# Down weights with four neighbouring rows per partition, gate and up columns taken in the matching order

## The reference

```python
def _swiglu_ffn(x, wg, wu, wd):
    return jax.nn.silu(x @ wg) * (x @ wu) @ wd
...
top_w, top_i = jax.lax.top_k(probs, K)            # K = 6 of E = 64
gate = jnp.zeros((N, E), dtype=x.dtype).at[jnp.arange(N)[:, None], top_i].set(top_w)
for e in range(NS):                               # NS = 2 shared experts
    shared = shared + _swiglu_ffn(x, sWg[e], sWu[e], sWd[e])
for e in range(E):
    routed = routed + _swiglu_ffn(x, Wg[e], Wu[e], Wd[e]) * gate[:, e:e + 1]
out = (shared + routed + x)
```

## Time and profile before

| | us |
|---|---|
| median of 3 runs | 1272.34 (1271.11 to 1272.39) |
| profiled execution | 1267.19 |
| its span | 1265.8 |
| TensorE busy in the span | 980.7 (77%) |
| VectorE busy | 568.4 (45%) |
| DMA queue q1 (SyncE): share of the 16 DMA engines | 55.0% |
| mean rate of all DMAs | 255 GB/s |

### The profile page before, as it was taken

How to read it: one execution, slowest core, us unless ns; L and a number is a source line. 1 busy time by engine, 2 the same in 40 slices (tenths; PEclk the granted TensorE clock), 3 DMA queues, 4 the chain that set the end, 5 groups by cost and what they waited for, 6 DMA issues and landing times.

```text
span 1265.8 us, 20487 instructions
## 1 busy us (share of the span) xinstructions
PE 980.7 (77%) x7256; PEld 520.0 (41%) x7257; DVE 568.4 (45%) x1367; ACT 228.8 (18%) x582; POOL 372.2 (29%) x421
## 2 busy tenths in 40 slices
PE   0166757667676666776889999999899996999986
PEld 0023423333243332433654545455354543545463
DVE  5266859577595866996441111111111121111116
ACT  1021202122120321212311211112111120212100
POOL 1724041340414315000167322333223232232110
PEclk9997878887786978898577999999999997999998
DMA  7926061551605426056367999999999999999937
GB/s 245 326 73 253 15 266 62 205 202 66 266 34 232 155 113 261 6 200 226 130 196 245 318 391 381 387 393 384 392 384 389 390 379 399 384 382 388 371 106 205
DMA packets 92476, 322.76 MB, mean 255 GB/s; under 512 B 18395, under 2 KB 18548, under 8 KB 70322
## 3 DMA queue, kind: packets, MB, share of 16 engines
q1 hardware_dynamic: 68080, 259.90, 55.0%
q0 software_dynamic: 22432, 57.44, 12.9%
q10 hardware_dynamic: 1826, 3.54, 0.9%
HBM read 310.15 MB, written 13.63 MB: 256 GB/s over the span
## 4 chain that ended last, share of the span: by engine, by line
PE 67%; issue 11%; DVE 8%; DMA 3%; DVEq 3%; ACT 3%; another core or an unknown queue 2%; POOL 1%; SPq 1%; ACTq 0%; POOLq 0%
PE ps L1081 19%; PE ps L575 13%; PE ps L1125 10%; DVE big L558 5%; PE ps L1151 4%; PE ps L609 3%; PE ps L1031 3%; PE ps L625 3%; PE ps L1100 2%; PE ps L593 2%; DMA big<-y_d 2%; PE ps L1169 2%; DVEq L556 2%; PE ps L1075 1%
## 5 line engine op out<-in xcount | busy, mean ns | idle before, releaser
L558 DVE TENSOR_TENSOR big<-big 128x512 f32 x640 | 392.0, 694 | 156.7 <-remote 110.5
L575 PE MATMUL ps<-big,mixed 128*32 128x256 f32 x2560 | 219.5, 436 | 144.0 <-issue 97.0
L1081 PE MATMUL ps<-big 128*64 128x512 f32 x1024 | 248.2, 629 | 28.3 <-issue 27.2
L317 POOL DMA_INDIRECT big<-xn_d,idx x160 | 154.7, 967 | 342.8 <-DVE big L558 271.5
L575 PEld LDWEIGHTS ps<-big,mixed 128*32 128x32 f32 x2560 | 90.0, 121 | 266.0 <-issue 173.9
L1091 DVE TENSOR_TENSOR mixed<-big,ps 128x256 f32<-128x256 f32 x64 | 27.0, 421 | 295.3 <-ACT big L1088 291.3
L1081 PEld LDWEIGHTS ps<-big 128*64 128x64 f32 x1024 | 71.3, 144 | 163.5 <-issue 163.5
L1125 PE MATMUL ps<-big,mixed 128*64 128x256 f32 x1024 | 128.0, 393 | 1.6 <-issue 1.6
L981 POOL DMA_INDIRECT big<-h_d,Lg x52 | 50.9, 979 | 260.4 <-issue 258.9
L1048 POOL DMA_INDIRECT y_d<-big,sia x74 | 75.5, 1020 | 107.7 <-DVE big L1138 62.9
L584 ACT ACTIVATE mixed<-ps 128x512 f32<-128x512 f32 x40 | 23.9, 598 | 385.4 <-PE ps L575 359.9
(11 more groups left out here) (191 smaller groups left out, 728.7 us busy)
## 6 DMA issues: line engine op xcount, KB each, us to landing
big<-in_L_ffn_Wg SPq DMA_DIRECT2D x64, 1024.0 KB
big<-in_L_ffn_Wu SPq DMA_DIRECT2D x64, 1024.0 KB
big<-in_L_ffn_Wd SPq DMA_DIRECT2D x64, 1024.0 KB
big<-in_edge_attr SPq DMA_DIRECT2D x10, 4096.0 KB
big<-y_d SPq DMA_DIRECT2D x10, 672.0 KB
big<-xn_d,idx POOLq DMA_INDIRECT x160
big<-in_L_ffn_sWg SPq DMA_DIRECT2D x2, 1024.0 KB, 5.0
big<-in_L_ffn_sWu SPq DMA_DIRECT2D x2, 1024.0 KB, 7.1
```

Of the source, the lines that this page charges most:

```text
L317: pool.indirect_dma_start(xs[s][:, c, :], None, xn_d[:, :], bass.IndirectOffsetOnAxis(ap=table[:, c0 + c:c0 + c + 1], axis=0)).then_inc(x_ ...
L558: ins = dve.tensor_tensor(pr[k % 2][:, :, EXT * p:EXT * (p + 1)], xs[s][:, :, ds(o1, EXT)], es[s][:, :, ds(o2, EXT)], ALU.mult)
L575: ins = pe.matmul(bank(BA)[WIN * h:WIN * (h + 1), h0:h0 + HP * EXT], onehot[s][:, CW * h + r, :], pr[k % 2][:, CW * h + r, :], start=r == ...
L1081: ins = pe.matmul(bank(k2)[TA * h:TA * (h + 1), :].rearrange("p (w f) -> p w f", w=2), xgT[k2][:, k, 0:TA], gu[:, :, k, W * h:W * (h + 1)] ...
```

## The change

Wd is now loaded as `(p j)`: partition p gets the four neighbouring rows 4p to 4p+3 in one piece of 8 KB, as Wg and Wu do. Block j of the down product is then the hidden elements 4c+j for c from 0 to 127. So that the hidden layer comes out in that order, the gate and up products take their weight columns in another order. In the main part group h of the array takes the columns 4c+2h and 4c+2h+1, two neighbouring float32 of every four. In the tail group h takes column 4c+h, one float32 of every four. The results still lie side by side in PSUM. In the main part, neighbouring elements m = 0 and 1 of `hid` now belong to different blocks, so the two transposes of the main part read every second element of it; the tail's transpose is put ahead of them. The load of the shared experts' down weights is as before.

```diff
     def load_down(e, k):
         gu, d = weights(k)
-        sync.dma_start(d, w_down[ds(e, 1), :, :].rearrange("a (j p) d -> p (a j) d", p=P)).then_inc(d_in[k], 16)
+        sync.dma_start(d, w_down[ds(e, 1), :, :].rearrange("a (p j) d -> p (a j) d", j=FT)).then_inc(d_in[k], 16)
...
             for k in range(KT):
                 for h in range(4):
                     pe.matmul(bank(BC)[TC * h:TC * (h + 1), 0:2 * W].rearrange("p (w f) -> p w f", w=2),
-                              xgT[k2][:, k, TA:TB], gu[:, :, k, W * h:W * (h + 1)],
+                              xgT[k2][:, k, TA:TB],
+                              gu.rearrange("p w k (c j) -> p w k j c", j=FT)[:, :, k, h, :],
                               start=k == 0, stop=k == KT - 1)
-        W = F // 2
         for k in range(KT):
             for h in range(2):
-                ins = pe.matmul(bank(k2)[TA * h:TA * (h + 1), :].rearrange("p (w f) -> p w f", w=2),
-                                xgT[k2][:, k, 0:TA], gu[:, :, k, W * h:W * (h + 1)],
+                ins = pe.matmul(bank(k2)[TA * h:TA * (h + 1), :].rearrange("p (w c m) -> p w c m", w=2, m=FT // 2),
+                                xgT[k2][:, k, 0:TA],
+                                gu.rearrange("p w k (c g m) -> p w k g c m", g=2, m=FT // 2)[:, :, k, h],
                                 start=k == 0, stop=k == KT - 1)
...
-        for c in range(3):
-            ins = pe.transpose(bank(BH)[:, P * c:P * (c + 1)], hid[k2][:, P * c:P * (c + 1)], ident[:, :])
+        pe.transpose(bank(BH)[:, 2 * P:3 * P], hid[k2][:, 2 * P:3 * P], ident[:, :])
+        for m in range(FT // 2):
+            ins = pe.transpose(bank(BH)[:, P * m:P * (m + 1)],
+                               hid[k2][:, 0:2 * P].rearrange("p (c m) -> p m c", m=FT // 2)[:, m, :], ident[:, :])
         ins.then_inc(ht_ok, 1)
```

## The result

| | us | |
|---|---|---|
| before, median of 20 runs | 1273.74 | 1264.29 to 1278.38 |
| after, median of 20 runs | 1278.01 | 1270.96 to 1282.73 |
| ratio after / before | 1.0034 | 95% interval 1.0018 to 1.0050 |
| profiled execution after | 1279.99 | span 1278.6 |

What follows compares the result with a forecast made beforehand. The DMA engines were taken to set the pace from 700 us to expert 59's product, TensorE after 1172 us. The load's 11.7 us, with products and transposes at nothing, gave 1272.34 - 11.7 = 1260.6 us, range 1253 to 1270 us.

Steps and rivals of the forecast that it cites:

- The step that failed: Gate and up products: operands jumping by 16 bytes cost nothing; upper bound 3.4 us per main product, 1.7 us per tail.
- (2): Tail products run at half pace, ten of 1.7 us more, eight in TensorE's slack: 1264 us; chance 0.07.
- (3): Main gate and up product L1081 streams slower in all 64 experts, 1464 us at double time; chance 0.09.
- The slack of 26.4 us: TensorE's idle time before L1081 from 700 to 1200 us, 14 waits for Wg and Wu.
- The load: Down loads of experts 8 to 58, in 8 KB pieces: 51 x 0.23 = 11.7 us gained.
- the ends 8.3 and 15.3: Bounds in us on the down load's gain: 0.16 us per load by wall clock, 0.30 by engine time.
- Rival (1): Down load's gain is small, other limits making up the short packets' loss: 1268 to 1272 us; chance 0.18.
- The covers: TensorE's waits exceed the 11.7 us gain, expert 46's giving 8.7 of 11.12 us; the DMA queue doesn't run dry.
- The transposes: Two of three hidden transposes load every second float32: at most 0.12 us per expert, taken as nothing.
- The time base: Profiled execution of 1267.19 us, with the median's 5.15 us above it carried over to 1272.34 us.

Runs made afterwards that it cites:

- e6: Changed kernel with the main product reading single elements 16 bytes apart and transposes matched; measured once, 1353.13 us, 217 us above the median of the kernel before beside it.
- e2: Changed kernel with the old down load, so only the column order differs from the kernel before; 1279.3 us, ratio 1.0040 to the kernel before.
- e4: Changed kernel in a third layout: Wd in two runs of 4 KB, main product on neighbouring columns, tail on every second; 1266.12 us, ratio 0.9931 to before.
- e5: Changed kernel with the main product back on neighbouring columns, tail still jumping; 1130.81 us against 1136.28 us for the kernel before, ratio 0.9961.
- e3: Changed kernel with the tail product back on neighbouring columns, main product in pairs; 1263.93 us, ratio 0.9917 to the kernel before.
- e1: Kernel before with only the new down load of 8 KB runs, columns as before; 1261.0 us, ratio 0.9893 to the kernel before.
- e8: The kernel before, unchanged, run again for a second profile; measured once, 1136.87 us.

## Why the prediction was wrong

**The step that failed** is "I take no cost, because both operands that jump by 16 bytes need at most one new piece of memory per 0.89 ns". I took it from the weight loads of the earlier trace rows, where a jump added 0.45 ns per column, and argued that the slow float32 stream had that to spare. The runs showed in its place a doubled stream for single elements, 7.41 / (8 x 512) = 1.81 ns per column against 0.89 (e6) and 3.81 against 1.93 us in the tail (e2), and 5% more for pairs, 3.84 against 3.65 us (e2). A load and a stream don't answer alike: the hidden transposes now load every second element in at least 194 ns, as slow as the every fourth of the earlier trace rows, while a moving operand at that stride of 8 bytes loses 5% (e4). The load of weights after the change:

```profile
L1102 PEld LDWEIGHTS ps<-ident,mixed x128: 194/203/230, 644.2 to 1226.5; 128*128 128x128 f32 x128
```

The Trainium skill's rule (page "SBUF — State Buffer", section "Door 1: the DMA port swizzle", SBUF "cachelines"), two hits on a line of 16 bytes for full bandwidth, is what the streams show, but for the 5% at two hits. I had it as a rival of 0.07, by a row that measures another thing. No run here reads a pair that lies across two such lines, so the runs agree with the rule and don't single out the line as the cause.

**The sum.** Slow tails and a slow main stream were rivals (2) and (3), each weighed alone. With the load's gain, neither alone makes the kernel slower than before; e5 (tails slow, main quick) and e3 (the reverse) are both faster. Rival (2), which is e5, was priced too low all the same: 1264 us, 8.3 below, against 5.5 us measured in the median and 1 to 2 in the stretch. Eight tails were to vanish in the slack, but in e5 7.0 us of waits are left, 4.1 of them at expert 46: a cost at other experts doesn't use up every wait. Over the expert stretch the slow tails and the slow main product together add 55 x 0.21 = 11.6 us and 10 x 1.88 = 18.8 us of TensorE's time, 30.4 in all. Against that the waits fell from 26.4 to 4.4 us, 22.0 us, and groups at half clock cost 5.9 us more than their 3.65 before (6.40 and 5.14 in the earlier trace rows and one of 5.35) and 1.3 after (the 5.16 above), 4.6 us. This leaves 3.8 us; measured were 2.3 us, and the other 1.5 us are not accounted for. The product that I had overlooked:

```profile
905.30 5.35 PE L1081 MATMUL ps<-big 128*64 128x512 f32 x16 [2.05 <-issue]
```

The slack of 26.4 us in the earlier trace rows was read rightly as the threshold; I didn't set both costs against it at once, with the load's gain spending 11.7 of it already.

**The load** was right in mechanism and size: 11.7 us forecast, 11.2 us in the expert stretch and 12.6 us in the median (e1), between the ends 8.3 and 15.3. The Trainium skill's rule on small descriptors (page "DMA: Bandwidth & Descriptors", section "Why small descriptors are slow (HBM only)") would have made 4.6 us by the estimate in the prediction, and the 11.2 us of e1 speak against it here. Rival (1) is out.

**The covers** held in sum, by another way than I wrote: in e1 the wait at expert 46 gave back only 1.1 us (11.12 to 10.04) and not the 8.7 it was to give "whatever the small ones did". When its product starts, e1 is 8.2 us ahead all the same, counted from the ninth product: the waits before it gave 5.0 us (9.6 to 4.6), and the product at expert 30 was no longer at half clock, 1.7 us. The transposes cost 0.03 us an expert, close to the nothing assumed, though not for the reason given: their loads took 57 ns more, the whole cost of a single element, and yet added almost nothing to the expert.

**The time base.** I took the first profile's 1267.19 us as the kernel's and carried the 5.15 us over to the median. It was a quick execution in its message part, which did no harm since the sum was a difference.

## What to carry to other kernels

When a layout is changed to please the DMA engines, count what the new order does to each operand that streams into TensorE: float32 read singly at 16 bytes halved the stream, in pairs or at 8 bytes it lost 5%. Sum all such costs against the one slack they share before calling any of them hidden. And try the layout in between: here two runs of 4 KB kept over half of the load's gain and cost TensorE almost nothing.

## What the runs showed that I had not expected

The weight load of a transpose is nearly as slow at a stride of 8 bytes (194 ns at least, 203 in the median, for 128 columns) as at 16 (195 and 218), against 137 and 140 for neighbours.

The kernel before took 1273.57 us beside e1 to e4 and 1136.28 us beside e5 to e8, without a change in the program. The record gives chip 14 for the first of these groups and chip 12 for the second. The expert stretch is the same, 491.7 and 491.0 us; the first product of an expert starts at 626.87 and 502.74. In the message part of the first profile VectorE stands idle for 110.5 us before its products, put down to something outside of the core's own engines:

```profile
DVE big L558 <- remote: 110.5, 11, 13.3
```

The profiles of after and of e1 to e4 have 114 us of it, that of e8 none. The kernel and the trace say more than this label. The products of a message block are made in eight parts, and all nine waits of over 7 us, 109 us together, come before the third of them, where the code waits until TensorE has used up the first (`part_used`). Here is TensorE ahead of the wait that ends at 184.40 us, one part at its usual pace and then the one waited for:

```profile
168.03 1.94 PE L575 MATMUL ps<-big,mixed 128*32 128x256 f32 x32
171.25 1.28 PE L575 MATMUL ps<-big,mixed 128*32 128x256 f32 x9 [1.28 <-issue]
172.86 0.62 PE L575 MATMUL ps<-big,mixed 128*32 128x256 f32 x4 [0.33 <-issue]
174.98 1.08 PE L575 MATMUL ps<-big,mixed 128*32 128x256 f32 x4 [1.50 <-issue]
177.12 1.08 PE L575 MATMUL ps<-big,mixed 128*32 128x256 f32 x3 [1.06 <-issue]
179.94 1.01 PE L575 MATMUL ps<-big,mixed 128*32 128x256 f32 x3 [1.74 <-issue]
182.07 3.22 PE L575 MATMUL ps<-big,mixed 128*32 128x256 f32 x9 [1.12 <-issue]
```

The 32 records of one part take 1.94 us and then some 14 us. In e8 TensorE takes two parts in 5.70 us without a gap, though the DMA engines are as busy there (share 1.01 from 180 to 188 us, against 0.96 from 171 to 184 us in the first profile):

```profile
183.37 5.70 PE L575 MATMUL ps<-big,mixed 128*32 128x256 f32 x64
```

So VectorE waits for TensorE, and TensorE stands between its own products for a reason that the profile doesn't name. What it is, and whether the other chip is why the second group is free of it, no run here shows; it stays open.
